# One-hot masks of both routings with the token tile innermost, and lane numbers spread by GpSimd

## The chip, the cores and the metric

The kernel runs on one core of one Trainium2 chip. The metric is the device time of one execution in microseconds (us); the time before is the median of three runs. The engines are named as in the profile: PE (TensorE, with its weight loads as PEld), DVE (VectorE), ACT (ScalarE), POOL (GpSimd) and SP (SyncE).

## The reference

A block of 2048 tokens of width 512 passes a mixture of experts (MoE), an attention-like layer, and the same MoE again; each takes the layernorm of x and adds to x:

```python
x = x + 0.5 * _L0_ffn_ref(_layernorm(x, axis=-1), L0_ffn_gate_w, ...)
x = x + _L0_attn_ref(_layernorm(x, axis=-1), L0_attn_Wq, ...)
x = x + 0.5 * _L0_ffn_ref(_layernorm(x, axis=-1), L0_ffn_gate_w, ...)
# _L0_ffn_ref: 8 experts, TOP_K 2, D 512, H 352
scores = xf @ gate_w.T + gate_b + bias
top_scores, top_idx = jax.lax.top_k(scores, TOP_K)
gates = jax.nn.softmax(top_scores, axis=-1)
comb = jnp.sum(jax.nn.one_hot(top_idx, E, dtype=gates.dtype) * gates[..., None], axis=1)
h = jax.nn.silu(jnp.einsum('td,ehd->teh', xf, w1) + b1)
y = jnp.einsum('teh,edh->ted', h, w2) + b2
out = jnp.einsum('ted,te->td', y, comb)
```

## The kernel before, in words

The 2048 tokens are 16 tiles (NT) of 128 (P). Each MoE phase (`ph` 0 and 1) has two stages. The **routing** finds the two experts of each token and gives each of its two visits a slot: the slots are grouped by expert, padded to whole tiles of 128, 39 tiles (SLOT_TILES) in all. The **slot loop** takes one slot tile after the other: GpSimd gathers its 128 rows from `xn_rows` in HBM by `slot_src` (line 574), PE transposes them (647), ACT and DVE split them in a high and a low 16-bit part (1094, 1519), PE multiplies by the expert's two weight matrices with ACT and DVE between, DVE scales by `slot_gate` (1538), and GpSimd scatters the rows to `y_rows` (578).

The order of the work on each engine is the order in which the code is written; semaphores tie the engines together. In the routing DVE goes through a long chain of small operations, each waiting for the one before (`seq`). It ends in a slot number per token and visit, split into `lo16` (place in the slot tile, 0 to 127) and `hi16` (number of the slot tile). To turn the map around, DVE makes one-hot masks in fp16: `OHlo` (lo16 against 128 lane numbers, line 1466), `OHhi` (hi16 against 39, 1468) and `OHtok` (OHhi times the token number, 1470), for both visits k. When they are done (`s_ohs`), PE multiplies OHlo by OHtok over 2 visits and 16 token tiles, 32 matmuls of 39 columns, each with an OHlo tile of 128 columns as its weights (call at line 710, recorded at 653). DVE makes `slot_src` of the result (1481 to 1483), and GpSimd waits for that to start the first gather. DVE then makes the gate masks `OHgate` (1499, four operations), and PE multiplies OHlo by them in `slot_gates`: 64 matmuls, placed after the first tile's up projection and the transposes of the second.

The first routing runs beside the loading of the expert weights. DVE splits experts 0 and 1 by itself (`split_low`, 1403 and 1406) just before the routing; PE makes the low parts of experts 2 to 4 with ACT (`low_piece`, 696 and 697). PE's `route(0)` does 11 such pieces ahead of its wait for the masks. They need the constants of GpSimd's `more_constants` (lines 537 and 565 to 569: `sel`, `unscale`, `minus`), which stand behind the four `std_of` of the layernorm (606) and ahead of `slots(0)`. In the second routing no such work lies beside the masks.

All operands of the masks are fp16. `lane16` is an fp16 copy of the lane numbers, made by DVE at line 1831 between the last layernorm offset (1634) and the splits. The masks lie as (visit, token tile, lane), so of the two inputs of an operation one has the step zero in the innermost dimension: `lo16` is repeated over the lanes.

Of the kernel before, what the change touches and what calls it, by code (L numbers as in the profile page):

```python
# [20 lines left out]
F32, F16, I32 = mybir.dt.float32, mybir.dt.float16, mybir.dt.int32  # L21
ACT = mybir.ActivationFunctionType
ALU = mybir.AluOpType
AX = mybir.AxisListType.X

P = 128
T, D = 2048, 512
E, HID = 8, 352
NT = T // P
# [3 lines left out]
SLOT_TILES = (2 * T + E * (P - 1)) // P  # L33
FW = KD * HID + KH * D
# [23 lines left out]
HI_PAD = SLOT_TILES + 1  # L58
# [40 lines left out]
def build(nc, x_in, ffn_w, gate_wT, gate_bias, b1, att_w, conv, rms_w, turns, out):  # L99
    ctx = ExitStack()  # L100
    with ctx:
        def sb(name, shape, dt=F32):
            return ctx.enter_context(nc.sbuf_tensor(name, shape, dt))

        def sem(name):
            return ctx.enter_context(nc.semaphore(name))
# [18 lines left out]
        desc = sb("desc", [P, NT, E])  # L125
        lane = sb("lane", [P, P])
        tokid = sb("tokid", [P, NT])
        lane16 = sb("lane16", [P, P], F16)
        tokid2 = sb("tokid2", [P, 2, NT])
        toks = sb("toks", [P, 2, NT], F16)  # L130
        ready = sb("ready", [P, 2, 2, NT], I32)
# [52 lines left out]
        lay = Layout(E * FW)  # L184
# [13 lines left out]
        late = Layout(late_at)  # L198
        OHlo, OHhi = [], []
        for at in (lay2, late):  # L200
            OHlo.append(at([2, NT, P], F16))
            OHhi.append(at([2, NT, HI_PAD], F16))
        OHtok = [lay2([2, NT, HI_PAD], F16)]
        assert lay2.at <= 0
        lay = Layout(late_at)
        apiece = lay([PIECE])
        OHgate = [lay([2, 2 * NT, HI_PAD], F16)]
        lay = Layout(max(late.at, moe_at + NCH * TPC * D + 2 * KD * PAIR))
        S, S2, OH1, OH2, KEY, M8, QP = (lay([NT, E]) for _ in range(7))
        raws_first = Layout(lay.at - 6 * NT * E)([PAIR], rows=E)  # L210
# [29 lines left out]
        x2_tail = lay([TPC, D])  # L240
        y_last = Layout(-ATT)([2, NT, D])
        rows_last = [lg[1][:, g] for g in range(NCH - 1)] + [x2_tail]
        OHtok.append(lay([2, NT, HI_PAD], F16))
        OHgate.append(lay([2, 2 * NT, HI_PAD], F16))
        assert lay.at <= E * FW

        group = TPC * D
        xT[0] = Layout(WEND)([2, KD, CH], F16)
        y_first = Layout(WEND)([2, TPC, D])
# [94 lines left out]
        c_first = sem("c_first")  # L344
        c_sum = sem("c_sum")
        s_ready = sem("s_ready")
        c_half = sem("c_half")
        yl_in = [[sem(f"yl_in{k}_{q}") for q in range(NT // 2)] for k in (0, 1)]
        f_pe = sem("f_pe")
# [178 lines left out]
        def _(gp):  # L528
# [32 lines left out]
            def more_constants():  # L561
                sel_rows = sel[:, :, :, :].rearrange("r t p (h c) -> r (t p h) c", h=2)
                for first in (0, 32):
                    select(sel_rows, sel_rows, ALU.not_equal, 1.0, -first, [[-1, NAB], [0, 64]], 1)
                seq(gp.memset(unscale[:, :], 0.0))
                seq(gp.affine_select(out=unscale[:, :], in_=unscale[:, :], compare_op=ALU.not_equal, fill=-UNSCALE, base=0,
                                     pattern=[[-1, P]], channel_multiplier=1))
                seq(gp.memset(minus[:, :], 0.0))
                gp.affine_select(out=minus[:, :], in_=minus[:, :], compare_op=ALU.not_equal, fill=-1.0, base=0,
                                 pattern=[[-1, P]], channel_multiplier=1).then_inc(consts, 1)  # L570
                gp.wait_ge(consts, 3)

            def gather(dst, rows, index, done):
                gp.indirect_dma_start(dst, None, rows, bass.IndirectOffsetOnAxis(ap=index, axis=0)).then_inc(done, 16)  # L574

# [28 lines left out]
            def std_of(n, par, lo=0, hi=TPC):  # L604
                gp.wait_ge(c_var, n + 1)
                gp.tensor_tensor(rstd[:, par, 0, lo:hi], nt4[:, 0, lo:hi], power[:, lo:hi, 0], ALU.pow).then_inc(c_pvar, 1)
# [6 lines left out]

            for g in range(NCH):
                std_of(g, g)
            more_constants()
            slots(0)
            for h in (0, 1):
# [18 lines left out]
                    add_out(c - 1, 3)  # L637
            for g in range(NCH):
                std_of(2 * NCH + 1 + g, g)
            slots(1)  # L640


        @block.tensor
        def _(pe):
# [55 lines left out]
            def route(ph):  # L700
                pe.wait_ge(s_onehot, ph + 1)
                chosen = M8.rearrange("p a b -> p (a b)")
                products(bank[3][:, 0:NT * E], [(before[:, :], chosen)])
                products(bank[4][:, 0:NT * E], [(ones[:, :], chosen)]).then_inc(s_count, 1)
                if not ph:
                    pe.wait_ge(consts, 3)
                    for n in range(2 * len(CUTS) - 1):
                        low_piece(OWN + n // len(CUTS), n % len(CUTS))
                pe.wait_ge(s_ohs, ph + 1)
                products(bank[5][:, 0:SLOT_TILES],  # L710
                         [(OHlo[ph][:, k, t, :], OHtok[ph][:, k, t, 0:SLOT_TILES]) for k in (0, 1) for t in range(NT)]).then_inc(s_inv, 1)

            def slot_gates(ph):
                pe.wait_ge(s_gates, ph + 1)
                products(bank[5][:, KH * P:KH * P + SLOT_TILES],
                         [(OHlo[ph][:, k, t, :], OHgate[ph][:, k, half * NT + t, 0:SLOT_TILES])
                          for k in (0, 1) for half in (0, 1) for t in range(NT)]).then_inc(s_slotg, 1)

            def slots(ph):
# [667 lines left out]
        def _(v):  # L1387
            ch = Chain(v, dve)

            def seq(ins):  # L1390

                ch(ins)
                ch.wait()
# [20 lines left out]
            def route(ph):  # L1414
# [47 lines left out]
                round_down(hi_f, posf, lo_f)  # L1462
                ch(v.tensor_copy(hi16, hi_f))
                seq(v.scalar_tensor_tensor(lo16, hi_f, -float(P), posf, ALU.mult, ALU.add))
                for k in (0, 1):
                    ch(v.tensor_tensor(OHlo[ph][:, k], lo16[:, k].unsqueeze(2).to_broadcast([P, NT, P]),
                                       lane16[:, :].unsqueeze(1).to_broadcast([P, NT, P]), ALU.is_equal))
                    seq(v.tensor_tensor(OHhi[ph][:, k, :, 0:SLOT_TILES], hi16[:, k].unsqueeze(2).to_broadcast([P, NT, SLOT_TILES]),
                                        lane16[:, 0:SLOT_TILES].unsqueeze(1).to_broadcast([P, NT, SLOT_TILES]), ALU.is_equal))
                    last = v.tensor_tensor(OHtok[ph][:, k, :, 0:SLOT_TILES], OHhi[ph][:, k, :, 0:SLOT_TILES],  # L1470
                                           toks[:, k].unsqueeze(2).to_broadcast([P, NT, SLOT_TILES]), ALU.mult)
                    if k == 0:
                        ch(last)
                last.then_inc(s_ohs, 1)
# [21 lines left out]
                    v.wait_ge(g_out[g], 16 * (ph + 1))  # L1496
                for k in (0, 1):
                    for half in (0, 1):
                        last = v.tensor_tensor(OHgate[ph][:, k, half * NT:(half + 1) * NT, 0:SLOT_TILES], OHhi[ph][:, k, :, 0:SLOT_TILES],
                                               gpart[:, half, k].unsqueeze(2).to_broadcast([P, NT, SLOT_TILES]), ALU.mult)  # L1500
                        if k + half < 2:
                            ch(last)
                last.then_inc(s_gates, 1)
# [324 lines left out]
            v.wait_ge(params, 16 * 4)  # L1828
            seq(v.tensor_tensor(gb[:, 0], gb[:, 0], gb[:, 1], ALU.add))
            offset(NCH - 1, NCH - 1, s_rstd)  # L1830
            ch(v.tensor_copy(lane16[:, :], lane[:, :]))
            ch(v.tensor_scalar(tokid2[:, 0], tokid[:, :], 2.0, -2.0 * T, ALU.mult, ALU.add))
            ch(v.tensor_scalar(tokid2[:, 1], tokid[:, :], -2.0, 2.0 * T, ALU.mult, ALU.add))
            for p in range(PAIRS):
# [73 lines left out]
```

## Time and profile before

| | us |
|---|---|
| median of 3 runs (lowest, highest) | 839.63 (839.11, 842.44) |
| profiled execution, its own time | 840.33 |
| its span | 838.6 |
| PE busy | 765.6 (91%) |
| DVE busy | 608.2 (73%) |
| ACT busy | 360.8 (43%) |
| POOL busy | 233.6 (28%) |

The span is the time from the first to the last instruction; 1.7 us of the execution's time lie outside it. A busy share is an average over stages that have different limits. PE is busy for 91% of the span, but in the routings it waits for DVE.

### The profile page before, as it was taken

The numbers are of one execution on the slowest core, as the hardware profiler recorded it, in microseconds if no ns is written. First come the engines' busy times: TensorE is split into PE (matmuls) and PEld (weight loads), VectorE is DVE, ScalarE is ACT, GpSimd is POOL, SyncE is SP. The second block draws the span as 40 slices with busy tenths as digits, with TensorE's granted clock in tenths as the row PEclk, the third lists the DMA queues.
The fourth block names the chain that finished last, engine by engine and source line by source line (L and its number), as shares of the span: only waits on it lengthen the run. The fifth ranks groups of instructions, "written<-read, shape, count | busy, mean of one in ns | idle before, by whom it ended". The sixth has DMA issues, their size and how long they took to land.

```text
span 838.6 us, 14107 instructions
## 1 busy us (share of the span) xinstructions
PE 765.6 (91%) x4218; PEld 423.7 (51%) x4219; DVE 608.2 (73%) x1024; ACT 360.8 (43%) x626; POOL 233.6 (28%) x225
## 2 busy tenths in 40 slices
PE   8688899999996998998999999999924999999998
PEld 5336455656563444444444444445513666666663
DVE  6885756666656569999989998896876555555557
ACT  5855333343433436445544654443260333333331
POOL 3212644445532001101211111102102444444432
PEclk9899999999997998899899999999976999999999
DMA  9974648974744701610352121265472573333698
GB/s 315 392 292 138 234 142 318 338 290 160 255 146 108 180 1 51 100 51 1 78 99 26 52 26 14 63 229 127 170 277 91 206 268 120 113 117 121 221 311 307
DMA packets 44955, 137.27 MB, mean 164 GB/s; under 512 B 5488, under 2 KB 5488, under 8 KB 41584
## 3 DMA queue, kind: packets, MB, share of 16 engines
q1 hardware_dynamic: 27536, 86.38, 28.7%
q0 software_dynamic: 17376, 50.34, 21.8%
q8 instruction: 24, 0.39, 0.2%
q14 instruction: 19, 0.16, 0.1%
HBM read 85.32 MB, written 51.38 MB: 163 GB/s over the span
## 4 chain that ended last, share of the span: by engine, by line
PE 77%; DVE 12%; ACT 3%; DMA 3%; issue 2%; POOL 2%; SPq 0%; DVEq 0%; ACTq 0%; POOLq 0%
PE bank L653 62%; PE bank L647 5%; PE bank L746 3%; DMA space<-xn_rows,slot_src 2%; PE bank L916 2%; PE bank L696 1%; PE bank L832 1%; DVE space L1406 1%; DVE space L1685 1%; POOL space L574 1%; DMA space<-x_in 1%; PE bank L850 1%; DVE space L1682 1%; DVE bst L1397 1%; ACT space L1147 1%
## 5 line engine op out<-in xcount | busy, mean ns | idle before, releaser
L653 PE MATMUL bank<-space 128*128 (+3 forms) x2958 | 580.5, 349 | 22.4 <-DVE space L1470 12.8
L653 PEld LDWEIGHTS bank<-space 128*128 128x128 f16 (+1 forms) x2958 | 276.3, 99 | 270.7 <-issue 25.4
L578 POOL DMA_INDIRECT y_rows<-space,slot_dst x78 | 89.2, 1144 | 158.3 <-DVE space L1538 157.7
L574 POOL DMA_INDIRECT space<-xn_rows,slot_src x78 | 81.7, 1047 | 121.7 <-PE bank L647 62.3
L1094 ACT ACTIVATE space<-bank 128x512 f16<-128x512 f32 x78 | 46.5, 597 | 145.3 <-PE bank L647 137.0
L1538 DVE TENSOR_SCALAR space<-bank,slot_gate 128x512 f32<-128x512 f32 x78 | 58.5, 750 | 60.3 <-PE bank L653 59.3
L1525 DVE SCALAR_TENSOR_TENSOR space<-bank,space 128x352 f32<-128x352 f32 x78 | 40.8, 523 | 59.3 <-PE bank L653 42.0
L1104 ACT ACTIVATE space<-bank 128x384 f16<-128x384 f32 x78 | 38.2, 489 | 94.5 <-PE bank L746 94.5
L647 PE MATMUL bank<-ident,space 128*128 128x128 f32 x440 | 66.5, 281 | 12.5 <-DMA space<-xn_rows,slot_src 10.6
L1519 DVE TENSOR_TENSOR space<-bank,space 128x512 f16<-128x512 f32 x78 | 53.9, 690 | 32.2 <-ACT space L1094 30.8
L1682 DVE SCALAR_TENSOR_TENSOR space<-space,cang 128x512 f32<-128x512 f32 x84 | 63.0, 750 | 5.5 <-ACT space L1186 3.3
L647 PEld LDWEIGHTS bank<-ident,space 128*128 128x128 f32 x440 | 54.3, 145 | 22.1 <-issue 12.0
L602 POOL TENSOR_TENSOR space<-space,power 128x8 f32<-128x8 f32 x12 | 23.8, 1985 | 144.0 <-ACT space L1214 144.0
L1186 ACT ACTIVATE space<-bank 128x512 f32<-128x512 f32 x48 | 28.5, 593 | 59.5 <-PE bank L653 59.5
L1685 DVE SCALAR_TENSOR_TENSOR space<-space,conv_sb 128x512 f32<-128x512 f32 x72 | 48.7, 745 | 0.0
L1530 DVE TENSOR_TENSOR space<-bank,space 128x384 f16<-128x384 f32 x78 | 43.1, 553 | 7.5 <-ACT space L1104 5.6
L1099 ACT ACTIVATE space<-space 128x352 f32<-128x352 f32 x78 | 38.2, 490 | 13.1 <-DVE space L1525 13.0
L746 PE MATMUL bank<-ident,space 128*128 128x128 f32 x234 | 39.4, 278 | 1.7 <-issue 1.5
L746 PEld LDWEIGHTS bank<-ident,space 128*128 128x128 f32 x234 | 28.5, 141 | 21.9 <-issue 11.8
L612 POOL DMA_DIRECT2D x_rows<-space x12 | 10.6, 882 | 100.5 <-ACT space L1237 100.5
L653 PE MATMUL bank<-space,gw 128*8 128x256 f32 x128 | 30.6, 382 | 0.6 <-ACT space L1086 0.6
L1397 DVE BATCH_NORM_STATS2 bst<-space 128x6 f32<-128x512 f32 x40 | 24.7, 678 | 1.8 <-DMA space<-x_in 1.8
(199 smaller groups left out, 747.3 us busy)
## 6 DMA issues: line engine op xcount, KB each, us to landing
space<-ffn_w SPq DMA_DIRECT2D x8, 1472.0 KB, 10.2
w_saved<-space SPq DMA_DIRECT2D x8, 1472.0 KB
space<-w_saved SPq DMA_DIRECT2D x8, 1472.0 KB, 9.1
xn_rows<-space SPq DMA_DIRECT2D x8, 1024.0 KB, 6.5
space<-y_rows SPq DMA_DIRECT2D x16, 512.0 KB, 6.5
space<-x_in SPq DMA_DIRECT2D x7, 1024.0 KB, 11.8
space<-att_w SPq DMA_DIRECT2D x12, 518.0 KB
space<-y_rows POOLq DMA_DIRECT2D x6, 1024.0 KB, 9.1
```

What stands on the lines that cost most here:

```text
L574: gp.indirect_dma_start(dst, None, rows, bass.IndirectOffsetOnAxis(ap=index, axis=0)).then_inc(done, 16)
L578: gp.indirect_dma_start(y_rows, bass.IndirectOffsetOnAxis(ap=slot_dst[:, t:t + 1], axis=0), yo[:, t % 2], None).then_inc(y_st[t % 2], 16)
L647: last = pe.transpose(dst[:, k * P:(k + 1) * P], src[:, k * P:(k + 1) * P], ident[:, :])
L653: last = pe.matmul(dst, a, b, start=(n == 0), stop=(n == len(terms) - 1))
L746: last = pe.transpose(bank[4 + par][:, c * P:(c + 1) * P], hact[:, par, c * P:(c + 1) * P], ident[:, :])
L1094: act.activation(xh[:, par], bank[par][:, :], ACT.Copy).then_inc(m_xh, 1)
L1519: v.tensor_tensor(xl[:, par], bank[par][:, :], xh[:, par], ALU.subtract).then_inc(m_xl, 1)
L1525: v.scalar_tensor_tensor(z[:, par], bank[2 + par][:, 0:HID], UNSCALE, b1_bc[:, bass.ds(ev * HID, HID)], ALU.mult, ALU.add).then_inc(m_zb, 1)
L1530: v.tensor_tensor(hl[:, par].rearrange("p a b -> p (a b)"), bank[4 + par][:, 0:KH * P], hh[:, par].rearrange("p a b -> p (a b)"), ALU.subt ...
L1538: v.tensor_scalar(yo[:, par], bank[6 + par][:, :], UNSCALE / GSCALE, slot_gate[:, bass.ds(t, 1)], ALU.mult, ALU.mult).then_inc(m_yo, 1)
L1682: seq(v.scalar_tensor_tensor(a, raw[:, p, kind, j:j + CH], cang[:, p, kind, j:j + 1], a, ALU.mult, ALU.add))
L1685: return ch(v.scalar_tensor_tensor(vcon[:, par, eo], raw[:, p, 2 + eo, j:j + CH], conv_sb[:, p, 2 + eo, j:j + 1], vcon[:, par, eo], ALU.mu ...
```

## The change

The masks are laid out as (visit, lane, token tile) with the 16 token tiles innermost: each lane's 16 values lie side by side. `lo16`, `hi16`, `toks` and `gpart` are read as rows of 16 that are repeated over the lanes, so their step of zero is in the outer dimension. The other input of OHlo and OHhi is no longer the 128 lane numbers but a tile `lanes` of 128 x 16 of them, each number 16 times, which GpSimd writes with one iota for each routing (`lane_numbers`). There are two such tiles, each in memory that is free at that time. The first is written between the four `std_of` and `more_constants`; the second behind the last four `std_of` and a wait for the attention's output products (`c_out`), ahead of `slots(1)`. DVE waits for it (`s_lanes`) ahead of the masks, and its copy `lane16` is gone. PE's operands have the same shapes, but the columns of a weight tile and those of the moving tile now lie 16 elements (32 bytes) apart, where they were adjacent.

```diff
-            OHlo.append(at([2, NT, P], F16))
-            OHhi.append(at([2, NT, HI_PAD], F16))
-        OHtok = [lay2([2, NT, HI_PAD], F16)]
+            OHlo.append(at([2, P, NT], F16))
+            OHhi.append(at([2, HI_PAD, NT], F16))
+        OHtok = [lay2([2, HI_PAD, NT], F16)]
...
-        OHgate = [lay([2, 2 * NT, HI_PAD], F16)]
+        OHgate = [lay([2, 2, HI_PAD, NT], F16)]
...
+        lanes = [Layout((E - 1) * FW)([P, NT], F16), Layout(35400)([P, NT], F16)]
...
+            def lane_numbers(ph):
+                count(lanes[ph], 0, [[1, P], [0, NT]], 0).then_inc(s_lanes, 1)
...
             for g in range(NCH):
                 std_of(g, g)
+            lane_numbers(0)
             more_constants()
             slots(0)
...
                 std_of(2 * NCH + 1 + g, g)
+            gp.wait_ge(c_out, NT)
+            lane_numbers(1)
             slots(1)
...
                 products(bank[5][:, 0:SLOT_TILES],
-                         [(OHlo[ph][:, k, t, :], OHtok[ph][:, k, t, 0:SLOT_TILES]) for k in (0, 1) for t in range(NT)]).then_inc(s_inv, 1)
+                         [(OHlo[ph][:, k, :, t], OHtok[ph][:, k, 0:SLOT_TILES, t]) for k in (0, 1) for t in range(NT)]).then_inc(s_inv, 1)
...
-                         [(OHlo[ph][:, k, t, :], OHgate[ph][:, k, half * NT + t, 0:SLOT_TILES])
+                         [(OHlo[ph][:, k, :, t], OHgate[ph][:, k, half, 0:SLOT_TILES, t])
...
+                v.wait_ge(s_lanes, ph + 1)
                 for k in (0, 1):
-                    ch(v.tensor_tensor(OHlo[ph][:, k], lo16[:, k].unsqueeze(2).to_broadcast([P, NT, P]),
-                                       lane16[:, :].unsqueeze(1).to_broadcast([P, NT, P]), ALU.is_equal))
-                    seq(v.tensor_tensor(OHhi[ph][:, k, :, 0:SLOT_TILES], hi16[:, k].unsqueeze(2).to_broadcast([P, NT, SLOT_TILES]),
-                                        lane16[:, 0:SLOT_TILES].unsqueeze(1).to_broadcast([P, NT, SLOT_TILES]), ALU.is_equal))
-                    last = v.tensor_tensor(OHtok[ph][:, k, :, 0:SLOT_TILES], OHhi[ph][:, k, :, 0:SLOT_TILES],
-                                           toks[:, k].unsqueeze(2).to_broadcast([P, NT, SLOT_TILES]), ALU.mult)
+                    ch(v.tensor_tensor(OHlo[ph][:, k], lo16[:, k].unsqueeze(1).to_broadcast([P, P, NT]), lanes[ph], ALU.is_equal))
+                    seq(v.tensor_tensor(OHhi[ph][:, k, 0:SLOT_TILES], hi16[:, k].unsqueeze(1).to_broadcast([P, SLOT_TILES, NT]),
+                                        lanes[ph][:, 0:SLOT_TILES], ALU.is_equal))
+                    last = v.tensor_tensor(OHtok[ph][:, k, 0:SLOT_TILES], OHhi[ph][:, k, 0:SLOT_TILES],
+                                           toks[:, k].unsqueeze(1).to_broadcast([P, SLOT_TILES, NT]), ALU.mult)
...
-                        last = v.tensor_tensor(OHgate[ph][:, k, half * NT:(half + 1) * NT, 0:SLOT_TILES], OHhi[ph][:, k, :, 0:SLOT_TILES],
-                                               gpart[:, half, k].unsqueeze(2).to_broadcast([P, NT, SLOT_TILES]), ALU.mult)
+                        last = v.tensor_tensor(OHgate[ph][:, k, half, 0:SLOT_TILES], OHhi[ph][:, k, 0:SLOT_TILES],
+                                               gpart[:, half, k].unsqueeze(1).to_broadcast([P, SLOT_TILES, NT]), ALU.mult)
...
-            ch(v.tensor_copy(lane16[:, :], lane[:, :]))
```

On POOL, from the constants of the start to the first gather, before (rstd<-nt,power is `std_of`; the rows from sel on are `more_constants`):

```order
L541 IOTA tokid 128x16
L606 TENSOR_TENSOR rstd<-nt,power 128x4 x4
L537 AFFINE_SELECT sel<-sel 44x768 x2
L565 MEMSET unscale 128x128
L566 AFFINE_SELECT unscale<-unscale 128x128
L568 MEMSET minus 128x128
L569 AFFINE_SELECT minus<-minus 128x128
```

and now:

```order
L542 IOTA tokid 128x16
L610 TENSOR_TENSOR rstd<-nt,power 128x4 x4
L542 IOTA space 128x2048
L538 AFFINE_SELECT sel<-sel 44x768 x2
L566 MEMSET unscale 128x128
L567 AFFINE_SELECT unscale<-unscale 128x128
L569 MEMSET minus 128x128
L570 AFFINE_SELECT minus<-minus 128x128
```

The iota of 2048 elements has come in ahead of `more_constants`, so that the four selects and two memsets stand later. On DVE, the same time, from the last offset of the layernorm to the start of the routing, before:

```order
L1634 SCALAR_TENSOR_TENSOR rstd<-mv,rstd 128x4
L1831 CAST lane<-lane 128x128
L1832 TENSOR_SCALAR tokid<-tokid 128x16
L1833 TENSOR_SCALAR tokid<-tokid 128x16
L1836 TENSOR_SCALAR cang<-conv_sb,turns_sb 128x4 x6
L1838 TENSOR_SCALAR c_now<-cang 128x3
```

and now:

```order
L1641 SCALAR_TENSOR_TENSOR rstd<-mv,rstd 128x4
L1838 TENSOR_SCALAR tokid<-tokid 128x16
L1839 TENSOR_SCALAR tokid<-tokid 128x16
L1842 TENSOR_SCALAR cang<-conv_sb,turns_sb 128x4 x6
L1844 TENSOR_SCALAR c_now<-cang 128x3
```

Only the cast of the lane numbers is gone; the rest of DVE's order is the same.

## Rows read from the trace of the kernel before

**Rows 1.** The page, chain that ended last: shares of the span by engine.
```profile
PE 77%; DVE 12%; ACT 3%; DMA 3%; issue 2%; POOL 2%; SPq 0%; DVEq 0%; ACTq 0%; POOLq 0%
```

**Rows 2.** Groups on DVE: shapes, xcount | busy us, mean ns | idle us before.
```profile
L1466 DVE TENSOR_TENSOR space<-space,lane 128x2048 f16<-128x2048 f16 x4 | 9.1, 2287 | 0.1
L1499 DVE TENSOR_TENSOR space<-space 128x624 f16<-128x624 f16 x8 | 5.9, 805 | 0.1
L1403 DVE TENSOR_SCALAR space<-space 128x2944 f16<-128x2944 f32 x2 | 3.4, 1684 | 0.0
L1470 DVE TENSOR_TENSOR space<-space,toks 128x624 f16<-128x624 f16 x4 | 3.2, 811 | 0.1
L1468 DVE TENSOR_TENSOR space<-space,lane 128x624 f16<-128x624 f16 x4 | 3.2, 803 | 0.0
```

**Rows 3.** Chain of waits, second routing and first slots: start us, us, what.
```profile
624.58 2.29 DVE space L1466
...
632.26 1.26 PE bank L653 x32
...
640.72 0.70 DVE space L1519
...
645.69 1.36 PE bank L653 x54
...
648.59 1.79 PE bank L653 x12
650.38 0.44 PE bank L647 x4
```

**Rows 4.** Timeline of ACT, second routing: start, us, instruction [idle before <-releaser].
```profile
639.83 0.60 ACT L1094 ACTIVATE space<-bank 128x512 f16<-128x512 f32 x1 [16.23 <-PE bank L647]
```

**Rows 5.** Windows: us, busy (x count) of each engine, granted PE clock, DMA share.
```profile
632.00:633.70 1.70, 1.25 (x32) 1.13 (x32) 1.34 (x5) 0.00 (x0) 0.00 (x0) 0.50 0.00 0
```

**Rows 6.** Chain of waits, first routing.
```profile
53.81 0.22 PE bank L697
54.03 0.82 PE bank L653 x32
...
56.58 6.64 DMA space<-xn_rows,slot_src
```

**Rows 7.** Timeline of DVE, first routing: the last mask.
```profile
52.48 0.81 DVE L1470 TENSOR_TENSOR space<-space,toks 128x624 f16<-128x624 f16 x1
```

**Rows 8.** Timeline of POOL, ahead of the first routing.
```profile
21.68 1.97 POOL L537 TENSOR_SCALAR_AFFINE_SELECT sel<-sel 44x768 f16<-44x768 f16 x2
...
24.81 1.64 POOL L569 TENSOR_SCALAR_AFFINE_SELECT minus<-minus 128x128 f16<-128x128 f16 x1
```

**Rows 9.** Timeline of DVE, the same stretch.
```profile
21.82 0.77 DVE L1634 SCALAR_TENSOR_TENSOR rstd<-mv,rstd 128x4 f32<-128x4 f32 x1 [1.10 <-POOL rstd L606]
...
24.61 1.68 DVE L1403 TENSOR_SCALAR space<-space 128x2944 f16<-128x2944 f32 x1
...
34.33 0.28 DVE L1424 TENSOR_TENSOR space<-bank,rstd 128x128 f32<-128x128 f32 x1
```

**Rows 10.** Timeline of PE around the start of the first routing.
```profile
33.29 0.29 PE L682 MATMUL bank<-ident,space 8*128 8x8 f32 x2 [0.52 <-ACT space L1086]
39.39 0.77 PE L653 MATMUL bank<-space,before 128*128 128x128 f32 x2 [5.81 <-DVE space L1441]
```

**Rows 11.** Groups on POOL: the iotas of the start.
```profile
L541 POOL IOTA desc<- 128x128 f32 x1 | 0.3, 350 | 0.1
L541 POOL IOTA lane<- 128x128 f32 x1 | 0.2, 238 | 0.1
L541 POOL IOTA tokid<- 128x16 f32 x1 | 0.1, 144 | 0.1
```

**Rows 12.** Groups of weight loads, shapes kept apart.
```profile
L653 PEld LDWEIGHTS bank<-space 128*128 128x128 f16 x2910 | 271.4, 98 | 257.3 <-issue 19.6 <-DVE space L1470 13.4
L647 PEld LDWEIGHTS bank<-ident,space 128*128 128x128 f32 x440 | 54.3, 145 | 22.1 <-issue 12.0 <-DMA space<-xn_rows,slot_src 3.5 <-ACT space L1197 1.2
```

More of the change, by code:

```diff
@@ L127, in build @@
         tokid = sb("tokid", [P, NT])
-        lane16 = sb("lane16", [P, P], F16)
         tokid2 = sb("tokid2", [P, 2, NT])
@@ L242, in build @@
         rows_last = [lg[1][:, g] for g in range(NCH - 1)] + [x2_tail]
-        OHtok.append(lay([2, NT, HI_PAD], F16))
-        OHgate.append(lay([2, 2 * NT, HI_PAD], F16))
+        OHtok.append(lay([2, HI_PAD, NT], F16))
+        OHgate.append(lay([2, 2, HI_PAD, NT], F16))
         assert lay.at <= E * FW
+        lanes = [Layout((E - 1) * FW)([P, NT], F16), Layout(35400)([P, NT], F16)]
         group = TPC * D
@@ L346, in build @@
         s_ready = sem("s_ready")
+        s_lanes = sem("s_lanes")
         c_half = sem("c_half")
```

## The prediction

> **What bounds the kernel now.** I read the page's chain that ended last first: PE holds 77% of it and DVE 12% [rows 1]. The masks are worth something only where that chain runs through them, so next comes the chain cut to the two routings, then the timelines of the engines around it, then the groups for durations.
>
> In the second routing the chain is DVE from the first mask at 624.58 us; PE starts its 32 products at 632.26 [rows 3] with a granted clock of 0.50 [rows 5], the lower level (1.2 GHz), after a long idle stretch. The chain then stays on DVE through the gate masks up to the first x_low at 640.72, and that instruction was late because DVE itself was: ACT had made its input by 639.83 + 0.60 = 640.43 [rows 3, 4].
>
> In the first routing it is not DVE. The last mask ends at 52.48 + 0.81 = 53.29 [rows 7], but PE is busy with its pieces of expert weights until 54.03 and goes from there straight into the 32 products; the first gather follows at 56.58 [rows 6]. Further ahead DVE is the limit again: PE sits idle 5.81 us until 39.39 for DVE's line 1441 [rows 10], and DVE reaches its routing at 34.33 without having waited [rows 9], 0.75 us after the scores were there (33.29 + 0.29 = 33.58, [rows 10]).
>
> **The masks on DVE.** A 2048-element mask takes 2287 ns, a 624-element one 803 to 811 [rows 2]. The slope is (2287 - 803) / 1424 = 1.04 ns per element and the fixed part 153 ns: one element per step. Line 1403 does 2944 elements in 1684 ns, (1684 - 153) / 2944 = 0.52 ns per element, two per step [rows 2]; it has one source and other types. Bounds for the new form: no change, or half the slope. I take half, as the operands are all fp16 and contiguous in the innermost dimension: 2048 x 0.52 + 153 = 1.22 us and 624 x 0.52 + 153 = 0.48. Per routing:
> - OHlo 2 x 1.07 = 2.13 us, OHhi 2 x 0.325 = 0.65, OHtok 2 x 0.33 = 0.66: together 3.44 us ahead of `s_ohs`;
> - OHgate 4 x 0.325 = 1.30 us behind it.
>
> The Trainium skill, "Vector Engine (DVE) Microarchitecture Reference", section 5.1, has just this pair: of a two-source operation on 2-byte data, one element read 16 times ran one per cycle, and a row read again and again ran two per cycle. The trace agrees with the first half (1.04 ns per element for each mask operation), and no row here shows the second.
>
> **Second routing: gain.** PE's products, `slot_src`, the gather, the transposes and ACT's copy move up by 3.44: ACT is done at 636.99, and x_low, 0.04 later, at 637.03. DVE itself is free at 640.72 - 3.44 - 1.30 = 635.98. So x_low comes 640.72 - 637.03 = 3.7 us earlier, and the next in line is no longer DVE but the gather's path. The slot loop behind it is tied to its own PE chain, so I let the 3.7 us pass to the end. The iota here costs nothing: it starts behind the last attention products and `std_of`, and DVE comes to the masks only at the end of its chain of small operations, which took some 11 us in the first routing (34.33 to 53.29 less 7.6 of masks). An iota of even 3.9 us (below) fits in that.
>
> **First routing: gain.** None. `s_ohs` comes 3.44 us earlier but PE reaches the products at 54.03 anyway. DVE's later 1.3 us are covered by the gather of 6.64 us [rows 6].
>
> **PE with columns 32 bytes apart.** The trace has no such operand. Adjacent columns: 54 pairs of weight load and 39-column product in 1.36 us, 25.2 ns a pair [rows 3], and 1.26 / 32 = 39 ns at the low clock. Lower bound: no difference. A guess with a basis: a 352-column fp16 product takes 1.79 / 12 = 149 ns, 0.42 ns per column; a 128-column fp32 transpose 0.44 / 4 = 110 ns, 0.86 per column [rows 3]. So PE seems to take 4 bytes per 0.86 ns, which holds two adjacent fp16 columns but only one of columns far apart: 39 x 0.86 = 33.5 ns a pair, 8.3 more than now; at the low clock, where a column takes at least as long anyway, nothing. Upper bound: the weight loads too go at one column per 0.86 ns, 128 x 0.86 = 110 ns a pair, 85 more. Between them lies an unpacked load as the fp32 ones are: 145 against 98 ns [rows 12], 47 more. I take 8.3 ns, the fp16 rows being the nearer ones. All three groups are on the chain: 32 + 64 pairs in the first phase and 64 warm ones in the second, 160 x 8.3 = 1.3 us (0.8 and 0.5), and the 32 cold ones nothing.
>
> The Trainium skill, "Advanced Engine Details and Errata", section SBUF Cachelines, speaks against the change: SBUF has lines of 16 bytes, and an access that goes to another line each time pays a penalty; 32 bytes is such a step. It names no price. If both streams paid as one column per 0.86 ns the sum would be the upper bound's, with the moving one alone the 1.3 us that I take.
>
> **The iota ahead of the constants.** 16 elements take 144 ns, 128 in one row 238, 128 in rows of eight 350 [rows 11]. By the first two 0.84 ns per element: 144 + 2032 x 0.84 = 1.85 us. Each short row adds 112 / 16 = 7 ns: with 128 rows of 16, 0.9 more, 2.75 us. By the third alone 1.84 ns per element: 3.9 us. I take 2.75. POOL itself has time: the constants were done at 24.81 + 1.64 = 26.45 [rows 8], and PE can't ask for them before 39.39 [rows 10]. What matters is DVE. At 21.82 its line 1634 took 0.77 us and ended with POOL's first select on `sel`; the last select, at 24.81, took 1.64 us and ended just behind line 1403 [rows 8, 9]. The two engines shut each other out for whole instructions. The iota pushes four selects to a later place: two on `sel`, 1.97 us together, and two on 128x128 tiles, which by the iotas of that size I estimate at 0.3 each; 2.4 to 2.6 us in all. Two ways give nearly the same:
> - it shuts DVE's small tensor_scalars out while it writes; then everything from 21.7 to 24.6 repeats 2.75 us later, less 0.1 for the missing cast: +2.65;
> - it lets them by; DVE gets to line 1403 earlier, is held there until 24.45, and the four selects then fit between the long splits, each holding DVE: 24.45 - 24.61 + 2.4 to 2.6 = +2.2 to +2.4.
>
> With nothing held by the iota and the selects between splits it is +0.5; with the iota at 3.9 us and the first way +3.8; below, the routing can't start earlier than 33.6, -0.7. I take +2.4. It is late at 34.33, so PE's first product, its 11 pieces and the gather are late by as much; nothing covers it.
>
> The Trainium skill, "SBUF — State Buffer", section Who interferes with whom, has DVE and GpSimd share one port pair, held for a whole instruction, and says that two-source DVE work doesn't meet a GpSimd instruction that only writes. By it line 1634 would go free of the iota, which is the second way; the sum is then the +2.2 to +2.4 above.
>
> **Sum.** First phase +2.4 + 0.8, second -3.7 + 0.5: 0.0 us. Against its own 840.33 the profiled execution would stay at 840.3; the median of the runs lies 0.7 lower, so 839.6 to 839.7. The forecast is no change: what is gained at the second routing is given back at the first and on PE.
>
> **The rivals.**
> - *PE pays for the weights* (slower). In `route` and `slot_gates` each load goes unpacked. At +47 ns, all 192 pairs: 9.0 us in place of my 1.3, 847.4; at +85 ns for the same pairs 16.3, 854.7. For it: the columns are as far apart as the fp32 identity's are wide apart, and more. Against: 98 ns of a load are mostly fixed, and load and product overlap, so that part may hide behind the 25 ns. It decides from about 30 ns a pair on.
> - *No collision in the first phase.* The iota ends early, the selects fall beside operations that don't mind: shift 0 or -0.7 in place of +2.4, 836.5 to 837.3. For it: the last select delayed nothing, it waited itself and line 1403 took its usual 1684 ns. Against: DVE's stretch from 24.6 to 34.3 has no gap for them.
> - *DVE stays at one element per step.* The change doesn't do what it says: the 3.7 us are missing, 843.4. For it: no two-source row of this trace runs at two per step. Against: none has contiguous fp16 on both sides.
> - *The gain in the second routing is lost to the gather.* The stores of `xn_rows` might still be running when the gather comes 3.44 us sooner. The DMA share is 0.00 from 632.0 on [rows 5]; the products would start at 628.8 and the gather, as in the first routing, 2.5 us behind (54.03 to 56.58), at 631.4. At most 0.6 us are at stake, and it gets no chance of its own.
>
> **How the numbers follow.** Forecast (837.5 to 842.5) 0.55; PE pays 0.20; no collision 0.15; DVE at one per step 0.10. Half a per cent is 4.2 us, about what a measurement of this kernel can tell from no change. Faster by more needs both ends at once, 0.04. Slower by more: nearly all of the PE rival, and a little of the others' upper ends, 0.24. Same 0.72. The range goes from 836.0, the no-collision case with a free PE, to 848.0, which takes in the nearer half of the PE rival.
>
> **What would show it.** Masks of 1.22 and 0.48 us; x_low of the second phase some 3.7 us earlier against the end of attention, with ACT as its releaser; the 54 pairs at 1.8 us in place of 1.36; the iota near 2.75 us; the first operation of the routing (line 1424 before) at 36.7 in place of 34.33. I am wrong if the pairs of the masks take over 55 ns, or if the splits at 24.6 start no later than now and have no gaps between them.

## The result, and the profile after

| | before | changed |
|---|---|---|
| median of 4 runs, us (lowest, highest) | 840.09 (839.11, 842.44) | 850.62 (848.96, 852.31) |
| profiled execution, its own time and span | 840.33, 838.6 | 849.49, 847.7 |

The changed kernel takes 1.0121 times the time of before, 95% interval 1.0089 to 1.0154: slower, by about 10 us. The forecast was 839.7 us and its range ended at 848.0; both are missed. The span grew by 9.1 us; the profiled execution is one of the two shorter of four, and the further 1.4 us in the median is not in the account below (the two longer executions had a mean granted clock of 0.952 and 0.953, the two shorter 0.956 and 0.957). Line numbers of the changed kernel are those of before plus 1 to 8 (the products' 653 is 660 now, 1466 is 1474); in the experiments they move a little again.

The shares of the chain hardly tell anything, and this is all that the page's summary says (against [rows 1]):

```profile
PE 76%; DVE 12%; ACT 4%; DMA 3%; issue 3%; POOL 2%; SPq 0%; DVEq 0%; ACTq 0%; POOLq 0%
```

The mask groups on DVE do what was forecast, 1.22 and 0.48 us (columns as in [rows 2]):

```profile
L1474 DVE TENSOR_TENSOR space<-space 128x2048 f16<-128x2048 f16 x4 | 4.9, 1222 | 0.1
L1506 DVE TENSOR_TENSOR space<-space 128x624 f16<-128x624 f16 x8 | 3.3, 478 | 0.1
L1477 DVE TENSOR_TENSOR space<-space,toks 128x624 f16<-128x624 f16 x4 | 1.9, 482 | 0.1
L1475 DVE TENSOR_TENSOR space<-space 128x624 f16<-128x624 f16 x4 | 1.9, 476 | 0.0
```

The chain of waits through the second routing (start us, us, what; against [rows 3]):

```profile
633.59 1.14 DVE space L1474
...
635.69 2.76 PE bank L660 x32
...
640.07 3.45 DMA space<-xn_rows,slot_src
...
644.78 0.60 ACT space L1101
...
645.51 0.70 DVE space L1526
...
646.44 3.43 PE bank L660 x12
649.87 0.44 PE bank L654 x4
650.31 5.05 PE bank L660 x64
655.35 0.67 PE bank L753 x3
656.03 3.52 PE bank L660 x12
```

Three things stand in it. The 32 products with OHtok take 2.76 us in place of 1.26, the 64 with OHgate 5.05 us in place of 1.77 in two pieces with 0.25 us between them, and the 12 products behind them, the second tile's up projection, 3.52 us in place of 1.79. Those last 12 read nothing that was changed. The chain of the first routing has the same three (against [rows 6]):

```profile
55.58 2.55 PE bank L660 x32
...
59.87 6.58 DMA space<-xn_rows,slot_src
...
71.33 4.73 PE bank L660 x64
76.05 0.55 PE bank L753 x3
76.60 3.25 PE bank L660 x12
```

Windows explain the last of the three (us, PE busy, granted clock, DMA share, GB/s). The clock goes to its lower level (0.50, 1.2 GHz) at the end of the 64 products in the first phase, at 76.0 us, and halfway through them in the second, at about 652.9. It comes back some 3.5 and 7 us later, though PE is busy all the time; before, it was 1.00 in both stretches:

```profile
71.00:76.00 5.00, 5.00 (x68) 1.00 0.84 336
...
77.00:79.00 2.00, 2.00 (x8) 0.50 0.00 0
...
650.00:652.00 2.00, 2.00 (x27) 1.00 0.49 94
652.00:654.00 2.00, 2.00 (x29) 0.72 0.87 365
654.00:656.00 2.00, 2.00 (x22) 0.50 0.93 391
...
660.00:662.00 2.00, 2.00 (x12) 1.00 0.52 106
```

Ahead of the first routing, POOL and DVE (timelines; against [rows 8, 9]):

```profile
22.69 2.47 POOL L542 IOTA space<- 128x2048 f16 x1
25.11 3.34 POOL L538 TENSOR_SCALAR_AFFINE_SELECT sel<-sel 44x768 f16<-44x768 f16 x2
```

```profile
22.83 0.16 DVE L1641 SCALAR_TENSOR_TENSOR rstd<-mv,rstd 128x4 f32<-128x4 f32 x1 [1.10 <-POOL rstd L610]
22.91 2.28 DVE L1838 TENSOR_SCALAR tokid<-tokid 128x16 f32<-128x16 f32 x1
...
27.73 3.80 DVE L1413 SCALAR_TENSOR_TENSOR space<-space 128x2944 f16<-128x2944 f32 x1
...
36.40 0.28 DVE L1431 TENSOR_TENSOR space<-bank,rstd 128x128 f32<-128x128 f32 x1
```

Reading one place after the other in both chains gives the shift of the changed kernel against before, and so the whole account:

| what | adds, us |
|---|---|
| the first inputs land later, before anything of the change runs (last `std_of` 20.71 to 21.72) | +1.0 |
| from there to the routing's first operation (34.33 to 36.40) | +1.1 |
| PE's pieces of weights between it and the products | -0.5 |
| 32 products, first routing (0.82 to 2.55) | +1.7 |
| 64 products, first routing (with their waits for the issue: 2.31 to 4.72) | +2.4 |
| next 12 products at the lower clock (1.79 to 3.25) | +1.5 |
| masks on DVE, second routing (products start 3.42 us less late) | -3.4 |
| 32 products, second routing (1.26 to 2.76) | +1.5 |
| 64 products, second routing (2.35 to 5.04) | +2.7 |
| next instructions at the lower clock (12 products 1.79 to 3.52, transposes) | +1.9 |
| all other stretches | -0.8 |
| sum | +9.1 |

The first and the third line of this table are not the change's doing. In the twelve traces of this case the last `std_of` starts at 20.50 to 21.72 us, and the stretch from the routing's first operation to the products takes 18.9 to 20.0 us, in no relation to what was changed. Here PE's clock rose during the second pair of its pieces (1.18 us in place of 1.70), which is the half us of the third line. The two lines on the 64 products of before include 0.53 and 0.57 us of waits for the issue, which are gone in the changed kernel: the products themselves grew by 2.9 and 3.3 us.

### The profile page after: what moved, and what is told of

Same layout as the page of the kernel before. It is cut to its first block, busy times and chain, and to the rows that moved or that the text cites. A ratio compares the mean times of both kernels' runs of the same rounds, so it can differ in the third digit from the quotient of the medians.

```text
span 847.7 us, 14110 instructions
## 1 busy us (share of the span) xinstructions
PE 777.0 (92%) x4218; PEld 434.3 (51%) x4219; DVE 599.9 (71%) x1023; ACT 360.6 (43%) x626; POOL 245.7 (29%) x227
## 4 chain that ended last, share of the span: by engine, by line
PE 76%; DVE 12%; ACT 4%; DMA 3%; issue 3%; POOL 2%; SPq 0%; DVEq 0%; ACTq 0%; POOLq 0%
PE bank L660 61%; PE bank L654 5%; PE bank L753 3%; DMA space<-xn_rows,slot_src 2%; PE bank L923 2%; PE bank L839 1%; PE bank L703 1%; DVE space L1689 1%; DVE space L1413 1%; DMA space<-x_in 1%; DVE space L1692 1%; POOL space L578 1%; PE bank L857 1%; DVE bst L1404 1%; ACT space L1154 1%
## 5 line engine op out<-in xcount | busy, mean ns | idle before, releaser
L660 PE MATMUL bank<-space 128*128 (+3 forms) x2958 | 592.0, 355 | 18.3 <-DVE space L1477 9.3
L660 PEld LDWEIGHTS bank<-space 128*128 128x128 f16 (+1 forms) x2958 | 286.8, 102 | 267.3 <-issue 23.6
```

The costliest lines, as they stand in the source:

```text
L660: last = pe.matmul(dst, a, b, start=(n == 0), stop=(n == len(terms) - 1))
```

## The experiments

Times are medians where a kernel ran several times. The ratio is to runs of before on the same chip in the same job (their medians were 840.8 and 842.3 us). A time without a ratio comes from a single run and counts only for its trace.

**Which operand costs.** OHlo is the weights of the products, OHtok and OHgate are the moving tile. Each was put back alone into the layout of before; the other keeps the new one.

```diff
# e1_weights_apart: against the changed kernel
-            OHhi.append(at([2, HI_PAD, NT], F16))
+            OHhi.append(at([2, NT, HI_PAD], F16))
...
-  (OHlo[ph][:, k, :, t], OHtok[ph][:, k, 0:SLOT_TILES, t])
+  (OHlo[ph][:, k, :, t], OHtok[ph][:, k, t, 0:SLOT_TILES])
# and the same for OHtok, OHgate and their masks
```

> Only OHlo, PE's weight operand, has the new layout; OHhi, OHtok and OHgate, the moving operand, lie as before and are made from lane16 at one element per step. Theory (the weight load pays for columns 32 bytes apart): the pairs stay at 75 to 78 ns as in the changed kernel (64 of them in about 5.0 us), the granted clock falls again behind the gates, and the time is about 852 (the changed kernel's 850.6 and some 1.3 us for the slower small masks). Rival (the moving operand pays): pairs at 25 to 33 ns, no fall of the clock, time about 840.

Measured: 850.96 us. The 64 products of the second phase and the 12 behind them:

```profile
652.88 3.92 PE bank L661 x64
...
657.51 2.94 PE bank L661 x12
```

```diff
# e2_moving_apart: against the changed kernel
-            OHlo.append(at([2, P, NT], F16))
+            OHlo.append(at([2, NT, P], F16))
...
-  (OHlo[ph][:, k, :, t], ...
+  (OHlo[ph][:, k, t, :], ...
```

> The counterpart: only OHhi, OHtok and OHgate have the new layout, OHlo lies as before and is made at one element per step (2287 ns). Theory (the weight load pays): 25 to 33 ns a pair, at most the 8 ns of the prediction; no fall of the clock; time about 840. Rival (the moving operand pays): 75 ns a pair, time about 852. If both pay in part, the two runs' excesses over 25 ns add up to the 50 ns, or each reaches the larger of the two.

Measured: 853.16 us.

```profile
654.15 4.69 PE bank L661 x64
...
659.52 3.52 PE bank L661 x12
```

A pair takes 61 ns with only the weights apart, 73 ns with only the moving columns apart, and 74 to 80 ns with both. These are groups at a granted clock of 1.00: the first routing's 32 products in 1.95, 2.35 and 2.55 us, and the 64 of the changed kernel's first phase in 4.73. The 79 ns of its second phase is a mixture, as the clock fell halfway. At the lower clock the order is the same: the second routing's 32 take 39 ns a pair before, 68 with the weights apart, 79 with the moving columns, 86 with both. Either alone is enough to slow the products and to bring the clock down behind them (2.94 and 3.52 us for the next 12). The two costs do not add up. That fits weight loads that run beside the products (from 72 to 75 us of the changed kernel PE and PEld are both busy all the time), so that a pair costs nearly what the slower stream costs; no run tests this further. No theory that puts the whole price on one of the operands survives.

**How far apart.** The masks were laid out as (visit, group of token tiles, lane, tile of the group), with groups of 2, 4 and 8 token tiles. DVE still reads rows without a zero inner step, but rows of 2, 4 or 8; PE's columns lie 4, 8 or 16 bytes apart, and POOL's iota shrinks with the group.

```diff
# e4_groups_of_2 (G = 2), e5_groups_of_4, e6_groups_of_8: against the changed kernel
-            OHlo.append(at([2, P, NT], F16))
+            OHlo.append(at([2, NT // G, P * G], F16))
...
-                count(lanes[ph], 0, [[1, P], [0, NT]], 0)
+                count(lanes[ph], 0, [[1, P], [0, G]], 0)
...
+            def col(tile, t, n):
+                return tile[:, t // G, :].rearrange("p (l g) -> p l g", g=G)[:, 0:n, t % G]
```

> The masks in groups of two token tiles: (visit, pair of tiles, lane, 2). DVE's operands are contiguous in rows of two, PE's columns lie 4 bytes apart, and the iota has 256 elements. Both theories: masks at 1.22 and 0.48 us. Theory A (PE pays when each column is in another 16-byte line): 4 bytes are free, pairs at 25 to 27 ns, no fall of the clock, time about 836 to 837. Theory B (PE pays as soon as columns aren't adjacent, since it then can't fetch two at once): pairs well over 30 ns, time between 840 and 850.

Measured: 837.0 us, ratio 0.9948 (0.9932 to 0.9965). Groups on DVE, and the chain of the second routing:

```profile
L1487 DVE TENSOR_TENSOR space<-space 128x2048 f16<-128x2048 f16 x4 | 4.9, 1222 | 0.1
```

```profile
628.10 1.26 PE bank L661 x32
...
642.00 1.62 PE bank L661 x64
...
644.22 1.79 PE bank L661 x12
```

The whole gain on DVE is kept with rows of two, the pairs are back at 25 ns, and the clock stays up. This kernel is faster than before, by about half a per cent, as theory A had it. Some 0.7 us of it lie in the first phase's 64 products, which take 1.62 us here where before took 2.31 with its two waits for the issue; why those waits are gone is not shown. In the second phase as much is gained there and lost again at a later gather (see e9 below).

> As e4_groups_of_2, with groups of four token tiles: PE's columns lie 8 bytes apart, two of them in each 16 bytes. At 4 bytes a pair took 25 ns, at 32 bytes 75. Theory (only a column that is alone in its 16 bytes costs): 25 to 33 ns a pair, no fall of the clock, time about 837. Rival (the cost grows with the bytes read over): about 33 to 45 ns a pair, time 838 to 842.

Measured: 839.73 us. Its 64 products:

```profile
645.25 2.62 PE bank L661 x64
```

That is 41 ns a pair: the rival, a cost that grows with the distance, and not the theory.

> Groups of eight: columns 16 bytes apart, each alone in its 16 bytes. Theory: the same 75 ns as at 32 bytes, the clock falls behind the gates, time about 850. Rival (growing with the distance): about 45 to 55 ns a pair, time 842 to 846.

Measured: 851.98 us.

```profile
652.47 4.93 PE bank L661 x64
...
658.07 2.92 PE bank L661 x12
```

Here the theory was right and the rival wrong: 16 bytes cost what 32 do.

| bytes between columns (both operands) | ns per pair, warm | 12 products behind, us |
|---|---|---|
| 2 (before) | 25 | 1.79 |
| 4 | 25 | 1.79 |
| 8 | 41 | 1.79 |
| 16 | 77 | 2.92 |
| 32 (changed) | 74 to 80 | 3.52 |

The warm prices at 16 bytes and beyond are best read from the first routing's 32 products, at a granted clock of 1.00 throughout: 2.47 us at 16 bytes (e6), 2.55 at 32. The 64 of e6 shown above ran in part at the lower clock.

**The iota's place.** The first iota stands behind POOL's constants in place of ahead of them.

```diff
# e3_iota_behind: against the changed kernel
-            lane_numbers(0)
             more_constants()
+            lane_numbers(0)
```

> The changed kernel with the first iota behind the constants in place of ahead of them. Theory (the iota holds DVE's small tensor_scalars and pushes the selects into the splits): from the last layernorm offset to the first operation of the routing DVE takes 12.5 us as before the change in place of 13.6, and the time falls by about 1 us, from 850.6 to 849.6. Rival (the 1.06 us between the two traces there is chance, or the iota does the same harm at its new place, among the long splits): no change of that stretch, time 850.6.

Measured: 850.0 us, ratio 1.0097 (1.0072 to 1.0122). DVE's stretch from the last offset to the routing took 12.37 us, as before the change (12.51) and 1.2 us less than in the changed kernel (13.57), and the mask products started 1.2 us earlier than there (54.36 against 55.58). That the two figures agree is chance: the first inputs landed 0.7 us earlier here too (last `std_of` 21.01 against 21.72), and PE's pieces took 0.7 us longer. Yet the span was no shorter (848.2). The trace has the place where the products' 1.2 us went: behind the wait for the gather PE was at the lower clock (row of PE, and the window), and the four transposes took 1.09 us in place of 0.63 and the pieces behind them twice their time.

```profile
65.28 1.09 PE L654 MATMUL bank<-ident,space 128*128 128x128 f32 x4 [2.53 <-DMA space<-xn_rows,slot_src]
```

```profile
66.00:68.00 2.00, 2.00 (x5) 0.50 0.00 0
```

So the iota's cost on DVE is shown, but its share in the run's time is not: the intervals of both kernels overlap.

**The same gain with PE's layout untouched.** The masks stay as before, but the small inputs `lo16`, `hi16`, `toks` and `gpart` are written twice, each value next to itself, so that a mask reads rows of two equal values against two adjacent lane numbers. No iota.

```diff
# e7_twice: against before
-        hi16, lo16 = (lay([2, NT], F16) for _ in range(2))
+        hi16, lo16 = (lay([2, NT, 2], F16) for _ in range(2))
...
+            def two(tile):
+                return tile.rearrange("p t (l g) -> p t l g", g=2)
+            def each(x, n):
+                return x.unsqueeze(2).to_broadcast([P, NT, n // 2, 2])
...
+                    ch(v.tensor_tensor(two(OHlo[ph][:, k]), each(lo16[:, k], P), numbers(P), ALU.is_equal))
```

> The masks lie as in the kernel before (PE's columns adjacent) and no iota is added. lo16, hi16, toks and gpart are written twice, side by side, so that the mask operations read them as rows of two with the step one, repeated over the lane pairs. Theory (two per step needs no more than an innermost row of two): masks at 1.22 and 0.49 us, pairs at 25 ns, the first routing's start as before, the second routing 3.6 us shorter; time 836.0 to 836.5, at least as good as e4_groups_of_2. Rival (rows of two whose next row doesn't touch run at one per step): 839.9, like before.

Measured: 837.67 us, ratio 0.9962 (0.9949 to 0.9975): faster than before, by somewhat less than expected. The second routing gave what it should: its products start 15.55 us behind its first operation, where before took 18.96. In the profiled execution the first inputs landed 0.9 us later than in before (last `std_of` 21.62 against 20.71), which has nothing to do with the masks.

```profile
L1484 DVE TENSOR_TENSOR space<-space,lane 128x2048 f16<-128x2048 f16 x4 | 4.9, 1222 | 0.1
```

```profile
643.27 1.65 PE bank L653 x64
```

**What brings the clock down.** In the changed kernel the fall could belong to the columns being apart, or to PE doing thin products for several us. This kernel is before with 128 products of 8 adjacent columns more, ahead of each 64 gate products; their result is not used.

```diff
# e8_gates_thin: against before
+                for again in range(2):
+                    products(bank[5][:, KH * P + 64:KH * P + 64 + 8],
+                             [(OHlo[ph][:, k, t, :], OHgate[ph][:, k, half * NT + t, 0:8]) for ...])
```

> The kernel before, with 128 extra products of 8 columns (of the same adjacent operands, into an unused part of the bank) ahead of the 64 products of the gates in each phase. Theory (the granted clock falls because few columns pass through PE for some us, whatever the distance of the columns): the extra pairs take 25 ns each, 3.2 us, and the granted clock falls to 0.50 during or behind them as it does in the changed kernel; time 840 + 6.4 + about 3 us. Rival (the fall belongs to the columns being apart): the clock stays at 1.00, time about 846.5.

Measured: 851.99 us. Timeline of PE and windows in the first phase:

```profile
69.15 5.20 PE L653 MATMUL bank<-space 128*128 128x8 f16 x188
...
76.43 3.68 PE L653 MATMUL bank<-space 128*128 x12
```

```profile
72.00:73.00 1.00, 1.00 (x46) 1.00 0.92 380
73.00:74.00 1.00, 1.00 (x38) 0.55 0.56 212
74.00:79.00 5.00, 3.93 (x27) 0.50 0.02 7
```

With every column adjacent and DVE's part as before, the clock fell while the thin products ran, and the next 12 products took 3.47 us on the chain in place of 1.79. PE was idle for 1.1 us between the fall and those 12, which may have kept the clock down for longer. In the second phase it had no such idle time: there the clock was 0.70 from 656 to 658 us and 0.50 from 658 to 660, and the next 12 took 2.11 us. The fall needs no distance between columns. What the kernels with a fall have in common is the stretch of weight loads and few columns ahead of it.

**The gate products in PE's idle time.** They were on the chain with some 2.3 us in each phase. Here they stand in the first phase ahead of the first transposes, where PE waits for the gather, and in the second between the first transposes and the first up projection, where it waits for ACT and DVE.

```diff
# e10_gates_alone: against before; e9_twice_and_gates: the same against e7_twice
+                if not ph:
+                    slot_gates(0)
...                                     # transposes of the first tile
+                if ph:
+                    slot_gates(1)
...                                     # up projection of the first, transposes of the second
-                slot_gates(ph)
```

> The version with the four small inputs written twice (layout of before, masks at two elements per step), and in addition slot_gates moved on PE: in phase 0 ahead of the first transposes, where PE waits for the gather, in phase 1 between the first transposes and the first up projection, where PE waits for ACT and DVE. In before these 64 products stand on the chain with 2.35 us in phase 0 (67.93 to 70.41 less the wait for the start of the next) and 2.4 us in phase 1 (645.53 to 648.04). My theory (what counts in a routing is only what lies on PE's or DVE's chain; 1.6 us of warm or 2.5 us of cold products fit in idle time of 2.6 us in phase 0 and 1.87 us in phase 1): 2 us less in each phase against the version without the move, about 833.5 to 834.5 us, some 6.5 us below before (ratio 0.992). Rival (the work put in the idle time leaves PE at the lower clock at the start of the slot loop, or its cold products run past the arrival of the next input): nothing or at most 1 us gained, 836.5 to 838.

> Before with the move of slot_gates alone, masks as before. In phase 0 the gate masks end at 60.3 and the gather lands at 63.2, so the products fit: 2 us less. In phase 1 the gate masks end only at 640.7, when x_low starts, so the 64 products take 1.6 to 2.5 us from there and push the first up projection from 641.66 to 642.4 to 643.3: 0.3 to 1.3 us less in place of 2. Theory: 837 to 838 us, ratio about 0.996. Rival (the clock falls or the products run late in both): 839.5 to 841, no change.

Measured: e9 836.45 us, ratio 0.9935 (0.9922 to 0.9948), the lowest ratio of all, though its interval overlaps that of e4; e10 839.62 us, ratio 0.9970 (0.9960 to 0.9980). e9 gains less than the 0.992 expected; e10's interval just takes in the 0.996 of its theory. What the move gave in each phase is read from the traces. PE's timeline in e9, first phase:

```profile
60.77 1.78 PE L653 MATMUL bank<-space 128*128 128x39 f16 x64
63.42 0.66 PE L647 MATMUL bank<-ident,space 128*128 128x128 f32 x4 [0.87 <-DMA space<-xn_rows,slot_src]
...
70.43 1.96 PE L653 MATMUL bank<-space 128*128 x12 [0.87 <-DVE space L1537]
```

The products fit ahead of the transposes as expected. But from the mask products to the second tile's 12 it is 16.36 us (54.07 to 70.43), and without the move, in e7, it was 16.38 (55.15 to 71.53): nothing gained. The gate products had covered the time that ACT and DVE need between the two projections of the first tile; now PE waits for it (0.87 us behind DVE's line 1537, and 0.83 us at the transposes ahead). In the second phase, chain of e9:

```profile
636.07 2.13 PE bank L653 x64
638.20 0.42 issue
638.62 2.06 PE bank L653 x12
...
643.33 1.96 PE bank L653 x12
```

The 64 products run at the lower clock and end past the arrival of their successor's input, but they let the clock rise: the first up projection takes 2.06 us, where it took 3.70 in e7. From the mask products to the second tile's 12 it is 14.87 us against 15.94 in e7, 1.1 us gained. But most of that is lost a few tiles on, where the transposes now wait for their gather:

```profile
655.05 0.66 PE L647 MATMUL bank<-ident,space 128*128 128x128 f32 x4 [0.76 <-DMA space<-xn_rows,slot_src]
```

From the mask products to the products behind these transposes it is 27.08 us against 27.36 in e7 and 27.38 in before, so only 0.3 us of the move stay (in e10, with the same wait, 0.5). Between the two profiled executions, each counted from its first mask products, nothing is left of it. The ratios of e9 and e7 are further apart than that (0.9935 and 0.9962, from two jobs on different chips), and the traces do not show why.

## Why the prediction was wrong

**The masks on DVE: right.** 1222 and 476 to 482 ns against 1.22 and 0.48 us. The Trainium skill, "Vector Engine (DVE) Microarchitecture Reference", section 5.1, gave two elements per cycle for a row read again and again; the traces here agree, down to rows of two elements (1222 ns in e4 and e7).

**Second routing, gain: right in mechanism and size.** The 3.44 us ahead of the products came as 3.42, and x_low then waited for ACT's line 1101 as forecast. x_low starts 4.79 us later than before, and the routing's first operation 6.85 us later; with the 1.50 us of slower products taken off, x_low gained 3.56 us, where I had 3.7. I had put it 0.04 us behind ACT's end, for which no row stands; it was 0.13 (645.38 to 645.51).

**First routing, gain none: right.** The last mask ended at 51.93 us (51.45 + 0.48), and PE went from its pieces of weights straight into the products at 55.58.

**PE with columns 32 bytes apart: the step that failed.** I weighed three prices and took 8.3 ns a pair for the warm pairs and nothing for the cold ones, "the fp16 rows being the nearer ones". Measured were 49 ns for the first phase's 64 warm pairs (74 less 25), 54 in the first routing's 32 (2.55 and 0.82 us), and 47 for the cold 32 (2.76 against 1.26 us); the second phase's 64 came to 54, half of them at the lower clock. On the chain that is 8.3 us in place of 1.3, after the 1.1 us of waits for the issue that are gone. The premise was a rate of 4 bytes per 0.86 ns, taken from fp32 rows whose 4 bytes are adjacent. It says nothing of what columns far apart cost: with columns 4 bytes apart, where it asks for the same 8.3 ns, a pair cost nothing more (e4), and at 16 bytes 52 ns more (e6). The argument that the lower clock leaves room was wrong in the same way. The size is that of the rival *PE pays for the weights* (47 ns), to which I gave 0.20; but it was the rival by its price and not by its reason, since the moving tile alone costs as much or more (e2, 48 ns) as the weights alone (e1, 36 ns).

The Trainium skill, "Advanced Engine Details and Errata", section SBUF Cachelines, which speaks of lines of 16 bytes and a penalty where each access goes to another, had been put beside this step. The traces fit it from one side: 16 and 32 bytes cost the same, 77 and 74 to 80 ns. At 8 bytes, with two columns in each such line, part of the price is there already (41 ns).

**The clock: a term that was missing.** The forecast had no sentence on what PE's granted clock does behind the products. The fall cost 1.5 and 1.9 us, and e8 shows that it needs no columns apart. With it the rival's 847.4 falls short too: its 9.0 us for PE stand against 8.3 + 3.4 measured. The range's upper end of 848.0 had no room for this.

**The iota ahead of the constants: right in kind, too dear.** It took 2.47 us (forecast 2.75), and did both things that I had as alternatives: line 1641 went free of it (0.16 us), the small tensor_scalars behind were held (2.2 us), and the selects then fell beside the splits. I had +2.4 for the start of the routing; it was +1.06 beside 1.0 us of later inputs, inside the given bounds of -0.7 to +3.8. The reason is that DVE's small operations had been held before too, beside the first selects (0.77 and 1.61 us): from the last offset to the first split the iota added only 0.40 us (3.19 in place of 2.79). The splits added the other 0.66, most of it in one that took 3.80 in place of 3.23 us. PE's pieces gave half of the 1.06 back, by the luck of an earlier rise of the clock. POOL's selects paid most (`minus` 3.12 us in place of 1.64, `unscale` 2.81 in place of 0.31), and nobody waited for them.

**The sum** was 0.0 from +2.4, +0.8, -3.7 and +0.5; measured in the same places: +0.6 (iota less PE's pieces), +4.1, -3.4 and +4.2, then +3.4 for the clock, +1.0 of later inputs and -0.8 elsewhere: 9.1. One term carries the error, and one that was not there. The 1.0 us of later inputs and the half us of PE's pieces are luck.

## What to carry to other kernels

Before a tile's layout is turned for the engine that writes it, price the engine that reads it: here DVE won 3.4 us per routing, which counted only in the second, and PE lost 4 in each phase. Both could be had, with adjacent pairs (columns at most 4 bytes apart) or by doubling the small input, because DVE's double rate needs rows of only two. And when many small matmuls stand on the chain, look at the granted clock of what follows them as well as at their own time.

## What the runs showed of the hardware that was not expected

- PE's products of 39 fp16 columns with 128-column weights: 25 ns a pair at 2 and at 4 bytes between columns, 41 at 8, 77 at 16 and 74 to 80 at 32. Weights alone at 32 bytes 61, moving columns alone 73.
- DVE's fp16 operation with two tensors runs at two elements per step with rows of 2 elements whose outer dimensions have zero steps: 1222 ns for 128x2048, the same as with rows of 16.
- PE's clock fell to the lower level while the profile shows the engine as fully busy, during or at the end of groups of thin products that took 3.9 to 5.3 us (e1, e2, e3, e6, e8 and the changed kernel), and rose again under the up projection or the transposes that followed. With groups of 1.6 to 2.6 us (before, e4, e5, e7) it stayed up.
- Work put in PE's idle time at the lower clock let the following products run faster: 12 of them in 2.06 us in place of 3.70 (e9, against e7).
- An fp16 iota in two dimensions took 2.47 us for 2048 elements, 1.53 us for 256 (e4), 1.20 for 512 (e5) and 1.94 for 1024 (e6), while the fp32 ones of 128 elements take 0.24 and 0.35: the time does not follow the number of elements alone. Placed behind POOL's constants, beside DVE's splits, the same 2048 took 3.83 us (e3).
